# A fused feed-forward, attention, feed-forward block: the slots' bias made in TensorE, the last additions dealt to two engines, and the steps' second normalisations made in ScalarE

## The reference

```python
x = x + 0.5 * ffn(layernorm(x))
x = x + attention(layernorm(x))
x = x + 0.5 * ffn(layernorm(x))

def ffn(h):
    query = h @ Wq.T                                   # 512 -> 64
    scores = (query @ Wr.T) @ (aux_keys @ Wr.T).T / sqrt(48) + log_rel      # 128 slots
    top = top_k(scores, 8)
    attn = query @ aux_keys[top].T / sqrt(64) + log_rel[top]
    aux = softmax(attn) @ aux_values[top] @ Wvd.T @ Wvu.T
    u = clip(0.5 * log1p(var(h)) / (mean(log1p(var(h))) + 1e-6)
             + 2.5 * sigmoid(gelu(h @ Wu1.T + bu1) @ Wu2.T + bu2), 0, 5)
    gate = sigmoid(gate_w1 * clip((u - 0.5) / 1.5, 0, 1) + gate_bias)
    return h + where(gate < 0.05, 0, gate) * aux
```

## Time and profile before

| | us |
|---|---|
| median of three runs (lowest, highest) | 1425.62 (1423.89, 1426.12) |
| the profiled execution | 1426.41 |
| its span, first to last instruction | 1423.6 |
| PE busy | 1351.8 (95%) |
| DVE busy | 1177.8 (83%) |
| ACT busy | 953.3 (67%) |
| POOL busy | 704.9 (50%) |

### The profile page before, as it was taken

The page is one execution under the profiler, slowest core; times in us unless marked ns, Lnnn a source line. Parts: engine busy times, 40 slices in busy tenths (PEclk is TensorE's granted clock), DMA queues, the critical chain, the costliest instruction groups (busy, mean ns, idle before and its releaser), DMA issues.

```text
span 1423.6 us, 25847 instructions
## 1 busy us (share of the span) xinstructions
PE 1351.8 (95%) x8474; PEld 754.3 (53%) x8604; DVE 1177.8 (83%) x2877; ACT 953.3 (67%) x2463; POOL 704.9 (50%) x596
## 2 busy tenths in 40 slices
PE   4779999998999999999999999999999999999995
PEld 3444555554455555555555555555555555555553
DVE  7887978889899887988878898889777798778657
ACT  5568777676677676667667667667666676666754
POOL 3376767677765344445545454435543454434321
PEclk8899999999999999999999999999999999999998
DMA  8466766787777566656567655657666677556443
GB/s 281 164 137 136 199 184 174 186 190 176 179 167 167 109 146 147 138 126 146 140 127 165 134 132 141 127 127 161 135 138 124 141 147 160 113 136 134 93 89 119
DMA packets 439828, 211.20 MB, mean 148 GB/s; under 512 B 382016, under 2 KB 383344, under 8 KB 439696
## 3 DMA queue, kind: packets, MB, share of 16 engines
q1 hardware_dynamic: 438144, 208.18, 63.6%
q10 hardware_dynamic: 1552, 1.38, 0.3%
HBM read 91.00 MB, written 25.17 MB: 82 GB/s over the span
## 4 chain that ended last, share of the span: by engine, by line
PE 70%; DVE 15%; ACT 5%; issue 4%; POOL 4%; DMA 1%; DVEq 0%; SPq 0%; ACTq 0%
PE PJ L1536 16%; PE PJ L1537 15%; PE PJ L1535 15%; DVE phl L1256 4%; PE PV L1708 4%; PE PV L1703 4%; PE PV L1704 4%; PE SC L1724 4%; PE SC L1722 4%; PE SC L1723 4%; POOL t L629 2%; ACT p L839 2%; DVE p L1246 2%; DVE t L1202 2%; DVE t L1200 1%
## 5 line engine op out<-in xcount | busy, mean ns | idle before, releaser
L651 POOL TENSOR_TENSOR oTl<-of,oTf 128x512 f16<-128x512 f32 x128 | 154.1, 1204 | 437.3 <-ACT oTf L831 437.1
L839 ACT ACTIVATE p<-p,mn 128x512 f32<-128x512 f32 (+3 forms) x512 | 280.9, 550 | 96.6 <-DVE mn L1246 96.5
L1256 DVE SCALAR_TENSOR_TENSOR phl<-p,ri,phl 128x128 f16<-128x128 f32 (+3 forms) x512 | 329.3, 683 | 0.0
L850 ACT ACTIVATE phl<-p,ri 128x128 f16<-128x128 f32 (+3 forms) x512 | 245.6, 550 | 4.1
L1535 PE MATMUL PJ<-XT,wsp 128*128 128x512 f16 x628 | 238.9, 380 | 4.0 <-DVE t L1202 3.9
L629 POOL TENSOR_TENSOR t<-t 128x512 f32<-128x512 f32 x158 | 201.7, 1277 | 77.3 <-DVE t L1202 76.8
L1536 PE MATMUL PJ<-XT,wsp 128*128 128x512 f16 x628 | 238.8, 380 | 0.0
L1537 PE MATMUL PJ<-XT,wsp 128*128 128x512 f16 x628 | 238.5, 380 | 0.0
L1246 DVE CUSTOM_DVE_ANT_0 p<-SC,maskw 128x512 f32<-128x512 f32 (+3 forms) x512 | 219.8, 485 | 2.1
L1536 PE MATMUL PJ<-wosp,oTf 128*128 128x512 f16 x512 | 194.0, 379 | 4.3
L634 POOL TENSOR_TENSOR qTl<-t,qTh 128x512 f16<-128x512 f32 x127 | 148.5, 1170 | 92.5 <-ACT qTh L815 92.5
(11 more groups left out here) (263 smaller groups left out, 2589.6 us busy)
## 6 DMA issues: line engine op xcount, KB each, us to landing
wsp<-kept SPq DMA_DIRECT2D x146, 256.0 KB, 3.0
wosp<-kept SPq DMA_DIRECT2D x96, 256.0 KB, 3.2
raw<-in_wqkv SPq DMA_DIRECT2D x48, 256.0 KB, 3.5
kept<-wsp SPq DMA_DIRECT2D x42, 256.0 KB, 2.5
raw<-in_wo SPq DMA_DIRECT2D x32, 256.0 KB, 4.4
kept<-wosp SPq DMA_DIRECT2D x32, 256.0 KB, 3.0
pTf<-phl SPq DMA_TRANSPOSE x256, 3.8
X<-in_x SPq DMA_DIRECT2D x3, 1024.0 KB, 9.8
```

Of the source, the lines that this page charges most:

```text
L839: ins = nc.scalar.activation(pt, pt, ACT.Exp, bias=mn[:, par, i:i + 1], scale=-1.0, accum_out=rs[:, par, i:i + 1])
L850: nc.scalar.activation(phl[:, par, high(i, 0):high(i, i) + 1:3, :], p[:, par, SOFF[i]:SOFF[i] + w].rearrange("p (k t) -> p k t", t=P), ACT ...
L1256: nc.vector.scalar_tensor_tensor(out=phl[:, par, low(i, 0):low(i, i) + 1, :], in0=p[:, par, SOFF[i]:SOFF[i] + w].rearrange("p (k t) -> p k ...
```

## The change

- **Slots' bias in PE.** For batch 0 of the first and batch 3 of the second feed-forward (apart()), PE adds the bias itself: one float32 product of a row of ones by the row lr2 opens the accumulation of each score tile. The scales 1/sqrt(48) and -1/sqrt(64) go into the score weights (fqb in place of fqs), so top() reads the tile from PSUM and take_scores() is left out there. The other tiles keep take_scores(), now without the scale. lr2 and fqb are made in query_factors(), where DVE now waits for ld_fs.
- **Last additions.** `odd` is 1, 3, 5, 7, 9, 11; banks and order of the last products, and the places of the additions on DVE and ACT, are new; POOL waits for the last top() before its additions. variance_of_squares(2, 4) stands between the first two normalisations.
- **Second normalisations in ACT.** For all tiles of the steps but (0,1,0) and (0,1,1), ACT makes X * rstd + nb in one activation just ahead of normal_hi(); shift() on DVE makes nb = -mean * rstd behind each deviation(). In the tables the attention norm's deviation is in step 23 (22), its tiles in 24 to 27 (22 to 25), their turns in 25 to 28 (23 to 26), bo's additions on POOL in 28 and 29 (26 and 27); the second feed-forward's tiles are in 9 to 12 (8 to 11); the auxiliary products and additions of tiles 0 to 3 are one in each of steps 18 to 21 (two in 18, two in 20).

```diff
-        18: [("AUX", 0, 0), ("AUX", 0, 1)], 20: [("AUX", 0, 2), ("AUX", 0, 3)]}
+        18: [("AUX", 0, 0)], 19: [("AUX", 0, 1)], 20: [("AUX", 0, 2)], 21: [("AUX", 0, 3)]}
...
-         22: [("std", 1, 0), ("nrm", 1, 0)], 23: [("nrm", 1, 1)], 24: [("nrm", 1, 2)], 25: [("nrm", 1, 3)]}
+         21: [("aux", 0, 3), ("mom", 1, 3), ("var", 1, 0)], 23: [("std", 1, 0)]}
...
-        23: [("turn", 1, 0)], 24: [("turn", 1, 1)], 25: [("turn", 1, 2)], 26: [("turn", 1, 3)]}
+        25: [("turn", 1, 0)], 26: [("turn", 1, 1)], 27: [("turn", 1, 2)], 28: [("turn", 1, 3)]}
...
-        + [(("AUX", 1, 1, n - 4), n) for n in (4, 5, 6)] + [(("ET", 1, 3, 0), 1)]
-        + [(("AUX", 1, n // 4, n % 4), k) for n, k in ((7, 7), (8, 3), (9, 0), (10, 2), (11, 4), (12, 5), (13, 6), (14, 7),
-                                                       (15, 3))])
+        + [(("AUX", 1, n // 4, n % 4), k) for n, k in ((5, 5), (7, 7), (4, 4))] + [(("ET", 1, 3, 0), 1)]
+        + [(("AUX", 1, n // 4, n % 4), k) for n, k in ((6, 6), (8, 0), (9, 3), (11, 5), (10, 2), (12, 4), (13, 7), (14, 6),
+                                                       (15, 0))])
...
-        odd = [1, 3, 5]
+        odd = [1, 3, 5, 7, 9, 11]
...
+            pool.wait_ge(r_mn[1], NT)
             for n in odd:
                 aux_add(n)
...
+            def normal(k, bb, i):
+                users = hb_users[i % 2]
+                j = users.index((k, bb, i))
+                if j:
+                    k_, b_, i_ = users[j - 1]
+                    act.wait_ge(ln_lo[k_], 4 * b_ + i_ + 1)
+                act.wait_ge(ln_nb, shifts(k, bb))
+                n = 4 * bb + i
+                nc.scalar.activation(normal_of(k, bb, i), X[:, n, :], ACT.Identity, bias=nb[:, k, n:n + 1],
+                                     scale=rstd[:, k, n:n + 1]).then_inc(ln_h[k], 1)
...
                 nc.vector.reciprocal(fqr[:, :], fqs[:, :]).then_inc(fs_dve, 1)
+                nc.vector.tensor_scalar(fqb[:, 0:1], fqs[:, :], RDIM ** -0.5, None, ALU.mult)
+                nc.vector.tensor_scalar(fqb[:, 1:2], fqs[:, :], -BOT ** -0.5, None, ALU.mult).then_inc(fs_dve, 1)
+                dve.wait_ge(ld_fs, 96)
+                nc.vector.tensor_copy(lr2[0:1, 0:NSLOT], lrb[0:1, :])
+                nc.vector.tensor_scalar(lr2[0:1, NSLOT:2 * NSLOT], lrb[0:1, :], -1.0, None, ALU.mult).then_inc(fs_dve, 1)
...
             normal(2, bb, 0)
+            variance_of_squares(2, 4)
             normal(2, bb, 1)
-            variance_of_squares(2, 4)
...
             select(3)
-            add(0)
-            add(2)
             learned(1, bb)
             gate_1(1, 12, NT, 4)
             inverse_sums(1, 12, NT, 4)
-            add(4)
-            add(6)
+            add(0)
+            add(2)
             dve.wait_ge(g_exd, 11)
             gate_2(1, 12, NT)
             e_lo(1, bb)
-            add(7)
+            add(4)
+            add(6)
             dve.wait_ge(g_exd, 12)
             gate_3(12, NT)
             scales(1, 12, NT)
-            for n in range(8, NT):
+            add(8)
+            add(10)
+            for n in range(12, NT):
                 add(n)
...
-                    mm3(score_bank(f, bb, 2 * j + t), qfh[:, ts], qfl[:, ts], bh[:, :], bl[:, :], True, True
-                        ).then_inc(r_sc[f], 1)
+                    dst = score_bank(f, bb, 2 * j + t)
+                    if apart(f, bb):
+                        mm(dst, ones[0:1, :], lr2[:, :], start=True, stop=False)
+                    mm3(dst, qfh[:, ts], qfl[:, ts], bh[:, :], bl[:, :], not apart(f, bb), True).then_inc(r_sc[f], 1)
```

More of the change, by code:

```diff
@@ L145 @@
 PREPARED = {"pe": ["rk", "rmat", "wqT", "u1T", "v2"], "act": ["rk", "wq sums", "wq rows", "wq", "b0", "b1", "wu1", "v2"],
-            "dve": ["wq scales", "wq", "b0", "b1", "u1T", "v2"]}
+            "dve": ["wq scales", "b scales", "lr2", "wq", "b0", "b1", "u1T", "v2"]}
 def prepared(engine, what):
@@ L249, in macaron_kernel @@
         fql, fqs, fqr = (sb(n, [P, 1], F32) for n in ("fql", "fqs", "fqr"))
+        fqb = sb("fqb", [P, 2], F32)
+        lr2 = sb("lr2", [1, 2 * NSLOT], F32)
         fwvdT = sb("fwvdT", [P, CC, VB], F32)
@@ L336, in apart, with taken @@
             return (f, bb) in ((0, 0), (1, B - 1))
+        def taken(f, bb):
+            return 4 * (bb - 1 if f == 0 else bb)
         def query_bank(f, bb, j):
@@ L356, in rope_index, with product @@
             return 5 * n if kind == "K" else 5 * n + idx + 1
-        odd = [1, 3, 5]
+        odd = [1, 3, 5, 7, 9, 11]
+        PRODUCTS = [4 * t[2] + t[3] for t, _ in TAIL if t[0] == "AUX"]
+        def product(f, n):
+            return PRODUCTS.index(n) + 1 if f else n + 1
         def odd_tile(f, n):
@@ L381, in consumed @@
             if kind == "SCR":
-                return r_use[a], 4 * bb + 2 * i + 2
+                if apart(a, bb):
+                    return r_mn[a], 4 * bb + min(2 * i + 2, APART[2] if (a, bb) == APART[0:2] else 4)
+                return r_use[a], taken(a, bb) + 2 * i + 2
             if kind == "SCT":
-                return r_use[a], 4 * bb + i + 1
+                return r_mn[a], 4 * bb + i + 1
             if kind == "HID":
@@ L1079, in take_scores @@
                 i0, i1 = tiles[0], tiles[-1] + 1
[L1080 to L1083, removed]
+                both = bank(("SCR", f, bb, i0 // 2)).rearrange("p (t n) -> p t n", t=2)
                 lr = lrb[:, :].unsqueeze(1).to_broadcast([P, i1 - i0, NSLOT])
@@ L1088, in take_scores @@
                     dve.wait_ge(r_t[f], 4 * bb)
[L1089 to L1092, removed]
-                                               op1=ALU.subtract).then_inc(r_use[f], i1 - i0)
+                nc.vector.tensor_tensor(rsc[:, ts, :], both[:, :, 0:NSLOT], lr, ALU.add)
+                nc.vector.tensor_tensor(asc[:, f, ts, :], both[:, :, NSLOT:2 * NSLOT], lr, ALU.subtract
+                                        ).then_inc(r_use[f], i1 - i0)
             def query_lo(f, bb, j=0):
@@ L1308, in score_weights_lo @@
                     dve.wait_ge(fs_act, prepared("act", f"b{k}"))
-                    nc.vector.scalar_tensor_tensor(out=bl[:, c], in0=whole, scalar=fqs[:, 0:1], in1=bh[:, c], op0=ALU.mult,
+                    nc.vector.scalar_tensor_tensor(out=bl[:, c], in0=whole, scalar=fqb[:, k:k + 1], in1=bh[:, c], op0=ALU.mult,
                                                    op1=ALU.subtract).then_inc(fs_dve, 1)
@@ L1332, in select_first @@
             def select_first(i):
-                take_scores(0, 0, (i,))
                 top(0, 0, (i,))
@@ L1407, in _ @@
                 for stage, k, bb, i in side(DVE_A, DVE_B, s):
-                    if stage == "nrm" and (k, bb, i) not in ((0, 1, 0), (0, 1, 1)):
-                        normal(k, bb, i)
                     if stage == "var":
@@ L1497, in select @@
             def select(*tiles):
-                take_scores(1, bb, tiles)
                 top(1, bb, tiles)
```

69 lines of the change are left out of this document (46 added, 23 removed).

## The result

| | median us | runs | lowest to highest |
|---|---|---|---|
| before, beside it | 1425.87 | 6 | 1423.89 to 1426.84 |
| changed | 1435.94 | 6 | 1431.55 to 1437.20 |

The ratio is 1.0067, with a 95% interval from 1.0055 to 1.0078: slower by 9.5 us, where I had forecast 1424.0 and a range up to 1428.7.

A forecast was written before the change was run, and what follows sets the result against it. PE's projections bound from 400 us on; only head, first batch's steps (DVE's softmax and rope) and tail could move the end. +2.0 - 4.0 + 0.4 = -1.6 us from 1425.6 gives 1424.0 us, range 1419.3 to 1428.7.

The forecast's parts named there:

- Head: 0 to 65 us, ahead of the steps: bias rows on DVE and bias products on PE lengthen it by 2.0 us.
- The bias products: Head's four score tiles on PE: one f32 one-row product each, 0.43 us a tile, 1.7 us in all.
- The clock's rise: Head: PE's clock doubles at 17.4 us as before; if later, the head would be up to +3.5 us.
- The wait for the small loads: Head: DVE stands from 10.5 to 13.0 us for the last load, starting the first query product 1.5 us later.
- rival 4: Head: the wait for the small loads costs nothing, the rest as forecast; 1422.8 us, chance 0.06.
- Steps: First batch's 32 steps, 65 to 405 us: moving normalisations from DVE to ACT cuts PE's waits, -4.0 us.
- the new wait for XT: First batch's end, near 375 us: PE waits some 0.8 us for a turned XT because the last turn comes later.
- Later batches: From 400 us on: projections bound PE, which never waits; 24 of 34 moved normalisations cost and bring nothing.
- rival 2: First batch: ACT takes the bound, its normalisations delaying exps(); 1431.8 us, half of the effect 1428.7; chance 0.14.
- Tail: From 1386 us: products end 0.5 us sooner, but the full stores' stream starts 0.4 later, so +0.4 us.
- Rival 3: Tail: the last addition sets the end, -1.6 us instead of +0.4; 1422.0 us, chance 0.07.
- Rivals 1: First batch: bound by DVE throughout, so the steps give 8.5 us; 1419.5 us, chance 0.27.

The follow-up runs named there:

- e4: The changed kernel with the f32 bias product over all 128 rows in place of one row: 1428.12 us, ratio 1.0017.
- e2: The changed kernel without the f32 bias product in the eight apart tiles, rows lr2 and their wait kept: 1425.93 us, ratio 1.0002.
- e1: The changed kernel with the wait for the small loads and the rows lr2 moved behind score_weights_lo(): 1433.47 us, ratio 1.005.
- p3: The kernel before with only the steps' second normalisations on ACT and the auxiliary additions one a step: 1426.51 us, ratio 1.0002.
- p2: The kernel before with only the tail's last additions dealt anew and normal(2, 3, 1) behind the second pair's variance: 1424.74 us, ratio 0.9994.
- f1: The kernel before with the tail's additions dealt anew and normalisations k = 0 and 1 on ACT; k = 2 and biases stay on DVE: 1424.36 us, ratio 0.999.
- f2: f1 with the biases in TensorE by two 16-bit products over 128 rows, their rows made late: 1424.81 us, ratio 0.999.
- e5: The changed kernel with the f32 bias product replaced by two 16-bit products of one row: 1428.38 us, ratio 1.0017.
- e7: e4 with the one-row f32 bias product in the tail's four tiles, 128 rows kept in the head: 1429.71 us, ratio 1.0023.
- e8: The changed kernel with the one-row f32 bias product in the head's four tiles, 128 rows in the tail's: 1430.12 us, ratio 1.0027.

## Why the prediction was wrong

**Head, forecast +2.0, measured +6.0, +3.9 and +7.5 in three profiles.** This is the step that failed. In the first profile the hidden product begins at 24.19 where I had 21.95, and gelu() at 28.30 where I had 24.7. Those 3.6 us are the first three terms: the product's price 1.2, the late rise 1.0, the fall 1.4. The row that I took the price from, with the one behind it:

```profile
24.33 1.12 PE L1756 MATMUL PV<-oTf,u1T 32*128 32x512 f32 x2
25.38 0.44 PE L1605 MATMUL PJ<-ident,asc 128*128 128x128 f32 x2
```

- *The bias products.* I priced one at 0.43 us, "the row of its type". With one row it is 0.73, outside my bounds; four are 2.9 us for 1.7. I took the nearest row of that type without asking for the shape, and I read it too low: from its start to the next one's are 1.05 us, and half of that is 0.53; I had taken off 0.27 for a drain that the next product doesn't wait for. That 0.43 is what e4 pays over 128 rows is luck. The Trainium skill, "TensorE: Matmul & The Clock Gate", section "Why this matters for your kernels", has a product of 32 rows take as long as one of 128. Here one row took longer, 0.73 for 0.43 us, and this product of 32 rows took 1.05, where twice e4's 0.43 is 0.86 (an estimate for 512 columns over 128 rows). The measurement decides.
- *The clock's rise.* The sum has it double "at 17.4 as before". In this profile it does so only behind the query products, which end at 19.35 for my 18.6, and the first score tile takes 1.32 us for 1.06. I had named this ("if the clock rises later, up to +3.5") and left it out of the sum. PE gets its first query product later, and what it did before the rise moved with it; the rise comes at 18.5 in the second profile and behind 20 us in the third.
- *The clock's fall.* I never asked whether it could fall again behind a busy PE. It did: 0.52 in 24:27, 0.50 in 26:30 of the third profile. The same page of the Trainium skill, section "What's actually happening", ties the clock to how busy PE has been. The records call PE busy in these stretches, so by that rule as I read it nothing should have fallen; e4 against the changed kernel shows that the number of rows decides here.
- *The wait for the small loads.* One profile had the last one land at 13.0 us, and I took it as fixed. In the ten traces with the rows made early DVE went on between 13.1 and 15.0 us, and the first query product started between 15.96 and 17.83, +1.4 to +3.3 for my +1.5. e2's trace has the wait without the products, and its head is 2.1 us longer than before; e1's points the same way. So rival 4, that the wait costs nothing, was wrong.

**Steps, forecast -4.0, measured -3.5 in the changed kernel, -2.6 in p3.** The mechanism was right, the size is known to some 1.7 us only (the trace of p2). PE's wait near 328 and its half clock went; the waits for turned probabilities in 160:400 are 8.1 us in eight pieces of at most 1.6; the new wait for XT is there, 0.9 us for my 0.8. My own sign for it, PE's idle in 300:400 from 7.8 to about 5 us, did not come: 7.4 remain. The gain lies before 300 us as well, and part of it is given back behind 345.

**Later batches, forecast 0, measured +2.6.** I wrote that there ACT is 69% busy and PE never waits, so "24 of the 34 cost and bring nothing". That PE never waits was true, but so narrowly that it bore no change: DVE's and ACT's chain of softmax and rope in steps 41 to 45 is hardly ahead of PE, and whatever PE gains before is waited away there. I took it for rival 2's mechanism in a place where I hadn't looked, the k = 2 normalisations on ACT; f1 shows that they aren't the whole cause, and how much of it they are stays open.

**Tail, forecast +0.4, measured +0.9 and +2.6.** Two terms were wrong with opposite signs. Dealing the additions is worth -1.6 by itself in p2's trace: e_hi() comes 1.8 us sooner relative to project_last(), not 0.2, and the stream of the stores starts 1.6 sooner, for my 0.4 later. The product costs 3.1 (e2's tail 39.4 us for 42.5), not 0.8, and in the third profile the clock takes 1.7 more. That full queues set the end held: in 1420:1428 they move 368 GB/s, and from DVE's last addition to the end are 6.5 us for 5.1. Rival 3 was wrong, although the -1.6 of p2 is its number: there DVE's last addition comes 3.0 us sooner and the end 1.6.

Rivals 1, 3 and 4 were wrong, and rival 2 too: the first batch gained. The sum failed for a mechanism that no rival held: none went slower through the head. My range ended at 1428.7, and the lowest of the changed kernel's 13 runs is 1430.26.

## What to carry to other kernels

Add a row vector in PSUM with a product over all 128 partitions (the row divided by 128, against ones, in 16-bit halves), not with a product of one row: here that is 0.22 us a tile for 0.73, and the clock held in its profile. Make what waits for a late load behind the work that doesn't need it: ahead of it, the wait cost this head some 2 us. Before a product is put into a short chain, ask what it does to the clock of the products behind it, above all where the work before and behind is short. And where a later stage never waits, look how far its second engine is from being late: what is gained ahead of it may be waited away there.

## What the hardware showed that I had not expected

- A f32 product of one row by 256 columns takes 0.73 us of PE with what it holds up around it, the same over 128 rows 0.43. The 16-bit form has gaps of some 0.1 us on either side as well: two passes cost 0.42 with one row, 0.22 with 128. The two passes of the f32 form start 0.32 us apart with one row and 0.22 with 128.
- The granted clock fell to 0.50 while PE's records are without a gap, behind one-row products, f32 or 16-bit, in head and tail. The profiles of e4 and f2, with the same work over 128 rows, and of e5, with two short passes, don't show it. Nor does the head of e7 or the tail's hidden product in e8, where the product is e4's.
- It does so in some executions only: of the six profiles with f32 one-row products in the head, two (the second of the changed kernel, and the bias alone) don't have it there. The spread of the runs alone is no sure sign of it. It was 5 to 7 us in most kernels with one-row f32 products but 2.5 in e1, and 2 to 3 in most without, but 4.8 in p2 and 4.6 in one set of the kernel before.
- The column of the granted clock read 1.00 from the start of the head, also where the distance of the products (0.21 us for 256 columns) was that of half clock. When the clock rose, by that distance, differed from 16.0 to behind 21 us.
- The same small load let DVE go on between 13.1 and 15.0 us in ten traces of nearly the same head.
